# Four-layer image network on one core: attention layer in smaller matmul pieces, deformable stages in one block

## The reference, cut to what matters

```
offsets = conv2d(x, ow, ob, K // 2)
out = deform_depthwise(x, offsets, dw, K, K // 2)
return conv2d(out, pw, pb, 0)
```

## Time and profile before

| | us |
|---|---|
| median of 3 runs (lowest, highest) | 6606.05 (6603.67, 6614.61) |
| the profiled execution's own time | 6606.96 |
| its span, first to last instruction | 6604.7 |
| TensorE busy (matmuls) | 5836.1, 88 % |
| VectorE busy | 4831.0, 73 % |
| ScalarE busy | 3905.2, 59 % |
| GpSimd busy | 782.4, 12 % |
| first and last exp of layer 0 | 108.5, 1924.8 |
| last output of layer 0 ends, first transpose of layer 1 | 1973.7, 2079.5 |
| last stage of layer 1 ends | 5605.3 |

### The profile page before, as it was taken

The page is one execution under the profiler, slowest core; times in us unless marked ns, Lnnn a source line. Parts: engine busy times, 40 slices in busy tenths (PEclk is TensorE's granted clock), DMA queues, the critical chain, the costliest instruction groups (busy, mean ns, idle before and its releaser), DMA issues. The chain is left out here.

```text
span 6604.7 us, 121718 instructions
## 1 busy us (share of the span) xinstructions
PE 5836.1 (88%) x45996; PEld 3998.1 (61%) x45996; DVE 4831.0 (73%) x10089; ACT 3905.2 (59%) x5362; POOL 782.4 (12%) x780
## 2 busy tenths in 40 slices
PE   5999999999977888988989989899889899699798
PEld 2554454454434556875568855588655688455598
DVE  6887887787765778887788877798777888344433
ACT  3766776676652557875567855578755787112142
POOL 2222211222202002001011000110100100000000
PEclk9999999999998999999989999999999899899898
DMA  4111111112104445545445545455544454211598
GB/s 145 43 56 55 40 44 55 49 39 59 44 23 134 105 105 123 124 110 118 105 117 118 119 97 129 99 126 121 117 105 108 114 124 111 96 46 41 145 234 199
DMA packets 198408, 651.46 MB, mean 99 GB/s; under 512 B 61753, under 2 KB 68849, under 8 KB 154915
## 3 DMA queue, kind: packets, MB, share of 16 engines
q1 hardware_dynamic: 177747, 604.65, 37.2%
q0 software_dynamic: 19968, 37.78, 2.2%
...
## 5 line engine op out<-in xcount | busy, mean ns | idle before, releaser
L2367 PE MATMUL b_p<-b_work,b_hkt 64*128 64x144 f32 (+37 forms) x27520 | 2116.5, 309 | 253.1 <-DVE b_acc L2238 149.7
L2367 PEld LDWEIGHTS b_p<-b_work,b_hkt 64*128 64x128 f32 x27520 | 1966.0, 195 | 479.9 <-DVE b_work L2313 283.2
L2313 DVE TENSOR_TENSOR b_work<-b_work 128x140 f32<-128x140 f32 (+26 forms) x5312 | 1605.5, 353 | 228.6 <-PE b_p L2367 174.7
L2208 ACT ACTIVATE b_work<-b_work,b_mcol 128x512 f32<-128x512 f32 (+6 forms) x1328 | 764.9, 647 | 1021.4 <-DVE b_work L2313 883.3
L530 ACT ACTIVATE a_ex<-a_p_t 128x1024 f32<-128x1024 f32 x512 | 523.9, 1023 | 427.3 <-PE a_p_t L466 424.5
L2212 ACT ACTIVATE b_work<-b_work,b_mrow 128x544 f32<-128x544 f32 (+6 forms) x1328 | 762.2, 645 | 0.0
L2238 DVE SCALAR_TENSOR_TENSOR b_acc<-b_p,b_dwc,b_acc 128x323 f32<-128x323 f32 (+14 forms) x1088 | 621.6, 574 | 184.5 <-PE b_p L2367 184.5
L596 DVE TENSOR_REDUCE a_nm<-a_p_x 128x1 f16<-128x1024 f32 x512 | 624.3, 1219 | 154.0 <-PE a_p_x L455 145.8
L1779 PE MATMUL b_p<-b_hp,b_ow 128*98 128x512 f32 x1568 | 721.4, 611 | 0.0
L602 DVE TENSOR_TENSOR a_el<-a_ex,a_eh 128x1024 f16<-128x1024 f32 x512 | 682.1, 1332 | 7.0 <-ACT a_eh L535 6.9
L535 ACT CAST a_eh<-a_ex 128x1024 f16<-128x1024 f32 x512 | 535.4, 1046 | 54.8 <-ACT a_ex L530 3.8
(11 more groups left out here) (224 smaller groups left out, 5811.6 us busy)
## 6 DMA issues: line engine op xcount, KB each, us to landing
...
d_win<-merged_kernels SPq DMA_DIRECT2D x192, 263.0 KB, 6.7
...
```

The lines of the kernel that those rows point to most:

```text
L2208: last = e.activation(rx[:, u, xo[c]:xo[c + 1]].rearrange("p (a b) -> p a b", a=H), pp[:, b, 1, :].rearrange("p (a b) -> p a b", a=H)[:, : ...
L2313: e.tensor_tensor(S[:, k % NS, 0:(r1 - r0) * w].rearrange("p (a b) -> p a b", b=w), rx[:, u, xo[cc]:xo[cc + 1]].rearrange("p (a b) -> p a ...
L2367: last = e.matmul(G[:, a0 - top:z0 - top, c0 - left:c1 - left], hkt[64 * s:64 * s + 64, SIDE * cr + cc, :], S[64 * s:64 * s + 64, k % NS, ...
```

## The change

- Layer 0: units take three slots for q and k (one matmul each) and two for values; two value units take one slot. Every slot from 26 to 74 has a piece. FIRST is 26, NORM_AT 86 and two images ahead. The product of a head's rows and its inverse moves to VectorE, into `o` of one head per parity; GpSimd then sends the rows by DMA into `packed`, 128 rows x 3 groups, so that an output half takes three matmuls instead of four, in pieces over two or three slots. Write-outs of VectorE follow in the slot behind. Loads of x and of the residual move in SP's queue.
- Layer 1: the offset convolutions start with the centre tap and skip rows and columns outside the image. layer1 gets an argument: as `near` all three stages of a pair stand in one block and the far sampler is left out; decide gathers one flag. Behind the layer this flag is tested, and if set the layer runs again in its old form (`far`). The accumulator's memset moves to GpSimd, turned_image's zeroing stays only in `far`.

```diff
-    FIRST = 14
-    BEGIN = -36
+    FIRST = 26
+    BEGIN = FIRST - STEPS
-    UNIT_AT = (28, 31, 34, 37, 40, 43, 45, 47, 50, 53, 56, 59, 62, 65, 78, 80, 82, 84, 86, 88)
+    UNIT_AT = ([tuple(range(m, m + 3)) for m in range(26, 38, 3)] + [(m, m + 1) for m in range(38, 46, 2)]
+               + [tuple(range(m, m + 3)) for m in range(46, 70, 3)] + [(70, 71), (72, 73), (74, 74), (82, 82)])
-    OUT_AT = (71, 72, 73, 75, 76, 77)
-    NORM_AT = 26
+    OUT_AT = ((75, 76, 77), (78, 78, 79), (80, 80, 81), (83, 83, 84), (85, 86, 87), (88, 88, 89))
+    NORM_AT = 86
+    PACK = [[(j, *piece[1:]) for j in range(G3) for piece in PIECES[j] if piece[0] == hd] for hd in range(HEADS)]
...
-                for g in ((0,), (1, 2))[part]:
-                    last = e.matmul(p_j[:], wqk[:, g, s, j * P:(j + 1) * P], h[:, g, n * HALF:(n + 1) * HALF], start=(g == 0), stop=(g == G3 - 1))
+                last = e.matmul(p_j[:], wqk[:, part, s, j * P:(j + 1) * P], h[:, part, n * HALF:(n + 1) * HALF], start=(part == 0), stop=(part == G3 - 1))
...
-                        if hh % HEADS in (1, 2):
-                            e.wait_ge(s_fo.sem, s_fo.at(b * (2 * G3) + hh // HEADS * (2 * G3) + hh % HEADS * G3))
+                        if hh % HEADS in (2, 3):
+                            e.wait_ge(s_fo.sem, s_fo.at((b + hh // HEADS) * (2 * G3) + (hh % HEADS - 1) * G3))
...
-                        for t in range(PAIRS):
-                            last = e.matmul(p_o[2 if i < 3 else 0][:], wp[:, t, g * P:(g + 1) * P],
-                                            o[:, t, n * HALF:(n + 1) * HALF], start=(t == 0), stop=(t == PAIRS - 1))
+                        last = e.matmul(p_o[0 if i < 3 else 2][:], wp[:, part, g * P:(g + 1) * P],
+                                        packed[:, part, n * HALF:(n + 1) * HALF], start=(part == 0), stop=(part == G3 - 1))
...
-                        e.tensor_tensor(o[r:r + D, hh // 2 % PAIRS, :], osum[r:r + D, :, :].rearrange("p n q -> p (n q)"), denb[r:r + D, :], ALU.mult).then_inc(s_n.sem, 1)
+                        for j, d0, d1, r in PACK[hh % HEADS]:
+                            e.dma_start(packed[r:r + d1 - d0, j, :], o[ROWS_OF[hh % 2] + d0:ROWS_OF[hh % 2] + d1, :]).then_inc(s_packed[hh % 2].sem, 16)
...
+                    k = m - 5 - BEHIND
+                    if ends_head(k, end):
...
+                        e.wait_ge(s_d4.sem, s_d4.at((b * HEADS + hh + 1) * 16))
...
+                        e.tensor_tensor(o[r:r + D, :], osum[r:r + D, :, :].rearrange("p n q -> p (n q)"), denb[r:r + D, :], ALU.mult).then_inc(s_n.sem, 1)
...
+    inner = K * K // 2
+    return [inner, *(tap for tap in range(K * K) if tap != inner)]
...
+            dy, dx = divmod(inner_first(K)[k], K)
+            up, left = dy - K // 2, dx - K // 2
+            (a0, z0), (a1, z1) = (max(0, -up - 16 * n), min(16, H - up - 16 * n)), (max(0, -left), min(W, W - left))
...
+                                hp[:, s, r0 + a0:r0 + z0, c0 + a1:c0 + z1], start=(k == 0), stop=(k == K * K - 1))
...
+            e.scalar_tensor_tensor(sh["anyfar"][:], fw[:], 0.0, sh["anyfar"][:], ALU.is_gt, ALU.max).then_inc(s_fl.sem, 1)
...
+                        elif g > 0:
+                            e.wait_ge(prev.s_ab.sem, prev.s_ab.at(2 * (last_in_slot(g - 1, b) + 1)))
...
+                        if g > 0:
+                            e.wait_ge(s_h8.sem, s_h8.at(pr * 3 + g + 1))
...
+                if K in QUARTERED:
+                    e.wait_ge(s_pw.sem, s_pw.at(stage * 4 + 4))
+                    e.sem_inc(sh["tick"], 1)
+                    e.memset(acc[:], 0.0).then_inc(tp.s_g.sem, 1)
...
+                    elif g > 0:
+                        e.wait_ge(prev.s_s.sem, prev.s_s.at(ITEMS1 * (LAST - 1 + tap)))
...
+                if g > 0:
+                    e.wait_ge(prev.s_g.sem, prev.s_g.at(sums_of(g - 1)))
+                sums_in_taps(e, gp)
...
-        layer1(nc, sh, x1, t, x2)
+        layer1(nc, sh, x1, t, x2, False)
+        with nc.If(nc.values_load(sh["again"][0:1, 0:1], min_val=0, max_val=1) > 0):
...
+            layer1(nc, sh, x1, t, x2, True)
```

787 lines of the change are left out of this document (433 added, 354 removed).

## The result

| | before | after |
|---|---|---|
| median, us (lowest, highest) | 6604.86 (6603.29, 6614.61) | 6353.53 (6336.03, 6355.39) |
| ratio, 95 % interval | | 0.9611 (0.9591 to 0.9630) |
| span of the profiled execution | 6604.7 | 6350.4 |
| first, last exp of layer 0 | 108.5, 1924.8 | 119.2, 1845.6 |
| first transpose of layer 1 | 2079.5 | 1993.5 |

A stage here runs from the end of its pointwise matmuls to its last sampling matmul, a seam from there to the end of the next pointwise matmuls. The kernel is 251 us faster; 6389 was forecast, some 36 above what came, and the runs of the two kernels do not overlap.

What follows compares the result with a forecast made beforehand. TensorE and VectorE were taken as nearly full in the attention layer, TensorE as fuller in the deformable one, both nearly empty between stages. Terms -69 - 70 - 79 - 4 + 4 = -218 took 6607 to 6389 us, range 6310 to 6478.

Steps and rivals of the forecast that it cites:

- Layer 0, -69 forecast: Attention layer: -9.4 us an image over 7 loops, last image -2, prologue +2, tail -3; sum -69 us.
- the 10.8 left over I take as unchanged: Attention layer: 222.3 us an image from summed loads against 233.1 measured; the remaining 10.8 was assumed to stay.
- The product's +2.1: Attention layer: VectorE pays 8 x 1.13 for the moved product and is rid of 8 x 0.86, +2.1 us an image.
- The 60 us that it rests on: Attention layer: VectorE's subtraction, mean 1.33 against median 1.21 us, 60 us over some 70 longer ones, laid to GpSimd's product.
- Convolutions, -70 forecast: Deformable layer: skipping columns and rows outside the image gives -59, -8 and -3, sum -70 us, bounds 0 and -90.
- One block, -79 forecast: Deformable layer's gaps: -6.9 x 4, -10 x 4, 3.5 x 3 between pairs, 1 at the end; bounds -50 and -95.
- the mark that was named for late positions: Deformable layer's stage starts: ScalarE's first hats of a stage only behind its start would mean positions came late.
- Memset, -4 forecast: Deformable layer: accumulator's memset (1.77 us) goes to GpSimd; TensorE starts some 1 us earlier in K=3, -4 us.
- Test, +4 forecast: Behind the deformable layer: a VectorE operation, a register load and a jump over the second copy; +4, bounded by 1.8 and 10.
- layer 0 gave more than nothing: Rival 1, attention layer: it gives nothing as VectorE's product and write-outs fall on TensorE; 6458 us, chance 0.22.
- More of each: Rival 2, whole kernel: the unevenness vanishes and convolutions pay in full; -277, 6330 us, chance 0.16.
- The product behind its landing: Rival 3, attention layer: VectorE's product waits for the inverse's landing and delays every slot; 6677 us, chance 0.04.

Runs made afterwards that it cites:

- that run: The changed kernel with the product of the rows and the inverse back on GpSimd: 6334.93 us, ratio 0.9587.
- held: The changed kernel with GpSimd made to start the K=7 stage's normalising only behind the pointwise sums at that stage's start: 6333.59 us, ratio 0.9587.

## Why the prediction was right, and where it was not

The time came out 36 us below the forecast and inside the range. The large terms came by the mechanisms that were named; that they came so near is in part luck, for a loss that was not foreseen (some 18 us at GpSimd) stands against gains that were not foreseen either (22 us in seams, by layer 0 alone). Term by term, by the profiled spans (-254.3, against -218):

- **Layer 0, -69 forecast, -82.7 came** (to layer 1's first transpose -86.0, of which its own start is -3.3). The period fell by 12.9, not 9.4; over all eight images that makes -90, the later first exp takes back 10.7, and the tail gives 3.5. TensorE's sum is as counted (-5.2 for -5.1). The step that failed is "the 10.8 left over I take as unchanged" (its sum of loads stands beside an image of 233.1 us; the mean is 233.9): the left-over and VectorE's excess are one thing, a few waits at known slots, and it fell by 7.7 (27.9 to 20.2) where 5.7 less 1.4 was put. The forecast's picture that evenness pays was half wrong: uneven projections cost 1.4 to 1.8 us an image, uneven outputs gain as much. The prologue cost 10.7, not 2: the unit more that stands ahead of the first exp takes ScalarE into the wait for moves (8.26 us), a DMA wait that a sum of matmuls doesn't show. The product's +2.1 held (2.0) by luck: VectorE is rid of 7.2 us an image in that run and not of 2.1, and most of it does not reach the period. The 60 us that it rests on were read rightly, but lie on 51 subtractions and not on some 70. Heads 2 and 3 behind the write-outs cost 2.6 us at slot 82, where 1.4 was set aside.
- **Convolutions, -70 forecast, -71 alone (62 by the stages), 72 in the changed kernel.** The K=3 and K=5 stages gave 53 us for the f32 ones against -59, the K=7 stage 8.9 for the f16 ones against -8. TensorE was indeed the engine that counts there: 53 of the 70 us of full columns came, 76 %, where 85 % was taken.
- **One block, -79 forecast, -105 in the seams and at the layer's end.** The two seams inside a pair closed to 7 us, below the 8.5 put together from parts: the transposes start at once, with no issue stall in front of them. The timeline of the K=3 to K=5 seam:

```profile
2940.91 2.92 DVE L2302 SCALAR_TENSOR_TENSOR b_near_acc<-b_near_p,b_near_dwc,b_near_acc 128x323 f32<-128x323 f32 x6
...
2942.05 1.10 PE L2400 MATMUL b_near_p<-ident,b_near_h 128*128 128x128 f32 x8
...
2945.05 2.32 ACT L2273 ACTIVATE b_near_work<-b_near_work,b_near_mcol 128x416 f32<-128x416 f32 x4 [19.62 <-DMA b_near_work<-sampling_positions_near]
...
2945.58 3.60 PE L1942 MATMUL b_near_p<-b_near_acc,b_near_pw 128*128 128x512 f32 x8
```

TensorE's transposes follow the last sampling matmul within 0.1 us. ScalarE's first hats, however, come only at 2945.05, held by a DMA of positions. "In one block ScalarE's first hats are done beforehand" did not hold here, and the mark that was named for late positions is there. It costs nothing in this seam, for 7 convolution matmuls stand ahead of the first sampling matmul (5.8 us behind the pointwise ones). The seam from pair to pair gave 5.2 each for 3.5, the layer's end 7.8 for 1 (its last store is issued 25.9 us behind the last sampling matmul instead of 33.7); of that 3.3 are left at the kernel's end. And 22.5 of the 48 us of the K=5 to K=7 seams come with the new layer 0 as well (75.7 to 53.2), at another granted clock: they may not be credited to the block, which leaves it about 82.

The rule of fetches ("Runtime: NRT & Kernel Launch", "Instruction fetch mechanics" of the Trainium skill) fits the issue stalls that went with the jumps (101.6 to 17.9 us, where the new layer 0 alone has 89.6). No run here shows a fetch as such.
- **Missed altogether**: taking the block's end away lets GpSimd run ahead. The K=5 stages lose 31.9 of the 41.6 us that cut convolutions give (1142.0 against 1110.1 held), the K=7 stages gain 14.3 of it back. Another 9.9 us of the K=7 stages (1764.4 with cut convolutions alone, 1754.5 held) have no term and no cause that a run shows. The prediction asked what SP's queue does when the barrier goes, and not what GpSimd's does.
- **Memset, -4 forecast, 15 to 18 us between the K=3 stages** (390.2 with cut convolutions alone and 393.1 with the memset back, 375.3 after). At the same time at half clock the difference is 0.5 to 3 us a stage, 2 to 12 in all; the rest goes with the clock and is not shown to be the memset's. It was costed as an operation of 1.77 us partly hidden; it was also a wait for the pointwise sums ahead of all products.
- **Test, +4 forecast, +3.3 measured** at layer 2's first transpose, nothing in the whole time.

The rivals: layer 0 gave more than nothing. "More of each" has a time (6330) nearer to what came (6353) than the forecast's, but not its conditions: 20.2 us of excess are left and the convolutions did not pay in full. The product behind its landing waits 4.6 us in all, and no sample was far. In layer 0 and in the seams the waits that the change removed were worth more than the forecast had put on them, and the one it added at GpSimd was not on the list.
